# Batches of two for the last units, later routing steps in the tail, and 24 units behind thirteen groups in place of 20 behind twelve

## What is computed

```
x = x + layernorm(attention(layernorm(x)))
logits = layernorm(x) @ Wg;  the two best of 8 experts per token, weights by softmax of the two
out_e  = relu(xn @ W1[e] + b1[e]) @ W2[e] + b2[e]
x = x + layernorm(sum over the two experts of weight_e * out_e)
```

## Time and profile before

| | us |
|---|---|
| median of 3 runs | 921.08 |
| lowest, highest | 917.64, 922.35 |
| the profiled execution | 916.07 |
| its span, first to last instruction | 914.3 |
| TensorE busy | 807.3 (88%) |
| VectorE busy | 750.5 (82%) |
| ScalarE busy | 666.7 (73%) |
| GpSimd busy | 531.4 (58%) |

### The profile page before, as it was taken

One profiled execution on the slowest core, in us unless ns is written; L12 is line 12 of the kernel. 1 busy time (PEld: TensorE's weight loads), 2 busy tenths in 40 slices (PEclk: granted clock), 3 DMA queues, 4 the chain that ended last, 5 costly groups with the idle time before them and its releaser, 6 DMA issues.

```text
span 914.3 us, 25168 instructions
## 1 busy us (share of the span) xinstructions
PE 807.3 (88%) x8010; PEld 681.0 (74%) x8010; DVE 750.5 (82%) x2262; ACT 666.7 (73%) x1629; POOL 531.4 (58%) x1026
## 2 busy tenths in 40 slices
PE   4599999999999999999999999997868799999990
PEld 2487787777777777777777777776658689999990
DVE  5677887999989899998989899888857658888881
ACT  4678887777878677787867778785456678777771
POOL 4244363455556556555655555563656767777775
PEclk9899999999999999999999999999979999999996
DMA  7100000010102021130103000000244366667640
GB/s 197 31 3 4 4 4 12 6 32 10 44 9 58 12 64 56 35 91 9 28 16 88 14 8 11 9 12 8 56 125 139 109 174 180 186 179 189 182 119 1
DMA packets 60301, 57.46 MB, mean 63 GB/s; under 512 B 17863, under 2 KB 43997, under 8 KB 60171
## 3 DMA queue, kind: packets, MB, share of 16 engines
q1 hardware_dynamic: 55211, 47.27, 19.9%
q0 software_dynamic: 4960, 8.58, 2.8%
HBM read 44.14 MB, written 19.99 MB: 70 GB/s over the span
## 4 chain that ended last, share of the span: by engine, by line
DVE 33%; PE 23%; issue 21%; POOL 13%; ACT 3%; DMA 3%; SPq 3%; POOLq 1%; DVEq 0%; another core or an unknown queue 0%; ACTq 0%
POOL out_dram L2243 6%; DVE mg L1050 5%; PE bank L878 5%; DVE xt L788 5%; POOL moe_y L2238 3%; DMA rows<-csplit 2%; DVE state L1077 2%; PE bank L675 2%; DVE y L1062 2%; PE bank L862 2%; DVE ob L1103 2%; SPq L1729 2%; PE bank L677 2%; PE bank L676 2%; DVE y L1059 2%
## 5 line engine op out<-in xcount | busy, mean ns | idle before, releaser
L1041 POOL TENSOR_TENSOR y<-y,zt 128x256 f32<-128x256 f32 x64 | 46.8, 732 | 185.7 <-issue 92.8
L962 ACT ACTIVATE m<-bank 128x512 f32<-128x512 f32 x128 | 69.1, 592 | 77.9 <-PE bank L864 77.8
L675 PE MATMUL bank<-thi,whi 128*128 128x512 f32 x224 | 105.2, 470 | 15.3 <-DVE cs L812 8.3
L2150 PE MATMUL bank<-moe_w,moe_hid 128*128 x728 | 108.0, 278 | 0.0
L2243 POOL DMA_INDIRECT out_dram<-moe_y,moe_token x91 | 91.2, 1003 | 20.6 <-issue 10.5
L2113 PE MATMUL bank<-moe_h_turned,moe_w_now 128*128 128x128 f32 x728 | 99.3, 281 | 0.0
L2150 PEld LDWEIGHTS bank<-moe_w,moe_hid 128*128 128x128 f32 x728 | 97.3, 194 | 0.0
L1050 DVE TENSOR_TENSOR mg<-bank,m 128x512 f32<-128x512 f32 x128 | 82.3, 685 | 17.3 <-PE bank L878 16.6
L2113 PEld LDWEIGHTS bank<-moe_h_turned,moe_w_now 128*128 128x128 f32 x728 | 91.4, 197 | 0.0
L2124 ACT ACTIVATE moe_hid<-bank,moe_w_now 128x128 f32<-128x128 f32 x224 | 63.9, 368 | 35.6 <-PE bank L2113 28.6
L677 PE MATMUL bank<-thi,wlo 128*128 128x512 f32 x224 | 89.6, 400 | 0.0
(11 more groups left out here) (260 smaller groups left out, 2356.4 us busy)
## 6 DMA issues: line engine op xcount, KB each, us to landing
moe_w_now<-pair_weights SPq DMA_DIRECT2D x91, 259.0 KB
moe_block_in<-pair_rows SPq DMA_DIRECT2D x91, 66.5 KB, 2.5
pair_weights<-in_L_ffn_W_dram SPq DMA_DIRECT2D x31, 128.0 KB
parts<-csplit SPq DMA_DIRECT2D x128, 4.0 KB
rows<-csplit SPq DMA_DIRECT2D x128, 4.0 KB
pair_rows<-spare_row SPq DMA_DIRECT2D x29, 66.5 KB
out_dram<-moe_y,moe_token POOLq DMA_INDIRECT x91
pair_rows<-xall,row_index POOLq DMA_INDIRECT x64, 2.6
```

What stands on the lines that cost most here:

```text
L675: PE.matmul(bank[:], whi[:, w], thi[:], start=True, stop=False)
L2150: mm = PE.matmul(o, hid[:, u % HID, k, n, :], w2[:, bass.ds(e, 1), n, :].rearrange("p o d -> p (o d)"), start=False, stop=n == FB - 1, ski ...
```

## The change

Six things change.

1. `SPLIT` is 13 in place of 12, and `EARLY` follows: 24 in place of 20. Group 12's four scatters count for the first share. Group 12's places step now also brings out the counts, and the first table is made from them where it was made before.
2. Group 13's `first` and `second` leave the last tile of the attention part and stand in `dve_tail` step 0; its places product moves to `pe_tail` step 2, its index to `dve_tail` step 2.
3. In the tail VectorE does group 14's `dve_post2` first; group 15's comes at step 2 in place of 3, and GpSimd's `pool_post2` and group 13's scatter at step 1 in place of 3. Group 15's turn comes a step earlier, its places at step 11 in place of 12, its index at 12 in place of 13, its scatter at step 12 in place of 13; the second table is made at steps 12 and 13.
4. VectorE takes the hidden layer of every second unit from unit 15 on (`BY_ACT`), before from unit 21 on.
5. From unit 84 (`FINE`) on the batches are of two units (84-85, 86-87, 88-89, and 90 alone), before 84-87 and 88-90. Their token numbers are made at the first unit's step, not two later.
6. From step 89 on norm and return run six steps behind in place of seven: step 89 takes two units.

```diff
-SPLIT = 12
+SPLIT = 13
 HALVES = ((0, SPLIT), (SPLIT, GROUPS))
 UNITS = (TOK + NPAIR * (P - 1)) // P
 EARLY = -(-(SPLIT * GT - NPAIR * (P - 1)) // P) // 4 * 4
...
         elif q == GROUPS - 3:
-            for step, when in zip(steps, ((g, 1), (g, 2), (g, 2), (g, 3), (g, 3), (g, 3), (g, 3), end, end)):
+            for step, when in zip(steps, ((g, 1), (g, 2), (g, 2), (g, 3), (g, 3), end, end, end, end)):
...
     def dve_tail(dve, step):
         if step == 0:
-            dve_route_index(dve, GROUPS - 3)
             dve_post2(dve, G_LAST - 1, static)
-        if step == 1:
+            dve_route_first(dve, GROUPS - 3)
+            dve_route_second(dve, GROUPS - 3)
             dve_post1(dve, G_LAST, 1, static)
             dve_post1_stats(dve, G_LAST)
+        if step == 1:
+            dve_route_stats(dve, G_LAST - 1)
         if step == 2:
-            dve_route_stats(dve, G_LAST - 1)
-        if step == 3:
             dve_post2(dve, G_LAST, static)
+            dve_route_index(dve, GROUPS - 3)
...
-        if step == 13:
+        if step == 12:
             dve_route_index(dve, G_LAST)
     def pool_tail(pl, step):
         if step == 0:
             pool_post2(pl, G_LAST - 1)
             pool_scatter_group(pl, GROUPS - 4)
-        if step == 3:
+        if step == 1:
             pool_post2(pl, G_LAST)
             pool_scatter_group(pl, GROUPS - 3)
...
-        if step == 13:
+        if step == 12:
             pool_scatter_group(pl, G_LAST)
...
+    BY_ACT = 14
     STEPS = -(-UNITS // 2)
-    QUADS = -(-UNITS // 4)
+    FINE = UNITS // 4 * 4 - 4
+    STARTS = list(range(0, FINE, 4)) + list(range(FINE, UNITS, 2)) + [UNITS]
+    QUADS = len(STARTS) - 1
...
     def by_act(u):
-        return u < EARLY or u % 2 == 0
+        return u < BY_ACT or u % 2 == 0
...
+    SHARES_AT = {STARTS[q]: q for q in range(QUADS)}
+    TOKENS_AT = {STARTS[q] + (2 if STARTS[q] < FINE else 0): q for q in range(QUADS)}
+    def normed_at(step):
+        return range(max(0, step - NORM_LAG + (step > FINE + 5)), min(UNITS, step - NORM_LAG + 1 + (step >= FINE + 5)))
...
-            if u in (13, 14):
-                dve_table(dve, 1, u - 13)
-            if u == 17:
+            if u in (12, 13):
+                dve_table(dve, 1, u - 12)
+            if u == 20:
                 dve_skip(dve, 1)
...
-        for u in range(UNITS + NORM_LAG + 1):
+        for u in range(UNITS + NORM_LAG):
             if u < UNITS:
                 att.pool_tail(pl, u)
-            if u % 4 == 2 and u // 4 < QUADS:
-                pool_tokens(pl, u // 4)
-                pool_share_sums(pl, u // 4)
-            if NORM_LAG <= u < UNITS + NORM_LAG:
-                pool_out(pl, u - NORM_LAG)
-            if u > NORM_LAG:
-                pool_return(pl, u - NORM_LAG - 1)
+            if u in TOKENS_AT:
+                pool_tokens(pl, TOKENS_AT[u])
+                pool_share_sums(pl, TOKENS_AT[u])
+            for v in normed_at(u):
+                pool_out(pl, v)
+                if v:
+                    pool_return(pl, v - 1)
+        pool_return(pl, UNITS - 1)
```

More of the change, by code:

```diff
@@ L1562, in tensor_program @@
         pe_out_tile(pe, T_LAST, T_LAST % 2, last=True)
-        fr = tail_front()
-        pe_route_places(pe, GROUPS - 3, fr)
     def tail_front():
@@ L1628, in pe_tail @@
         fr = tail_front()
-        if step == 1:
+        if step == 2:
+            pe_route_places(pe, GROUPS - 3, fr)
             pe_route_turn(pe, G_LAST - 1, fr)
@@ L1632, in pe_tail @@
             pe_route_logits(pe, G_LAST - 1, fr)
-        if step == 5:
+        if step == 4:
             pe_route_turn(pe, G_LAST, fr)
@@ L1637, in pe_tail @@
             pe_route_logits(pe, G_LAST, fr)
-        if step == 12:
+        if step == 11:
             pe_route_places(pe, G_LAST, fr)
@@ L1646, in act_tail @@
         if step == 1:
-            act_route_turn(act, G_LAST - 1, fr)
-        if step == 2:
             for k in range(2):
                 act_ln2(act, G_LAST, k)
+        if step == 2:
+            act_route_turn(act, G_LAST - 1, fr)
         if step == 3:
@@ L1654, in act_tail @@
                 act_route_scale(act, G_LAST - 1, k)
-        if step == 6:
+        if step == 5:
             act_route_turn(act, G_LAST, fr)
@@ L1664, in dve_tail @@
         if step == 0:
-            dve_route_index(dve, GROUPS - 3)
             dve_post2(dve, G_LAST - 1, static)
-        if step == 1:
+            dve_route_first(dve, GROUPS - 3)
+            dve_route_second(dve, GROUPS - 3)
             dve_post1(dve, G_LAST, 1, static)
             dve_post1_stats(dve, G_LAST)
+        if step == 1:
+            dve_route_stats(dve, G_LAST - 1)
         if step == 2:
-            dve_route_stats(dve, G_LAST - 1)
-        if step == 3:
             dve_post2(dve, G_LAST, static)
+            dve_route_index(dve, GROUPS - 3)
         if step == 4:
             dve_route_first(dve, G_LAST - 1)
+            dve_route_second(dve, G_LAST - 1)
         if step == 5:
-            dve_route_second(dve, G_LAST - 1)
-        if step == 6:
             dve_route_stats(dve, G_LAST)
@@ L1681, in dve_tail @@
             dve_route_index(dve, G_LAST - 1)
+            dve_route_first(dve, G_LAST)
         if step == 9:
-            dve_route_first(dve, G_LAST)
-        if step == 10:
             dve_route_second(dve, G_LAST)
-        if step == 13:
+        if step == 12:
             dve_route_index(dve, G_LAST)
@@ L1700, in pool_tail @@
             pool_scatter_group(pl, G_LAST - 1)
-        if step == 9:
             pool_route_norm(pl, G_LAST)
-        if step == 13:
+        if step == 12:
             pool_scatter_group(pl, G_LAST)
@@ L1834, in in_quad, with quad_with, in_quad_at @@
     def in_quad(q):
-        return range(4 * q, min(4 * q + 4, UNITS))
+        return range(STARTS[q], STARTS[q + 1])
+    def quad_with(u):
+        return u // 4 if u < FINE else FINE // 4 + (u - FINE) // 2
+    def in_quad_at(u):
+        return u - STARTS[quad_with(u)]
     def last_of(q):
@@ L2163, in pool_tokens @@
         pl.wait_ge(skip_ready.sem, 1 if last_of(q) < EARLY else 2)
-        PL.tensor_tensor(token_f[:, a:a + many], skip[:, 4 * q:4 * q + many], v[:, :, C_TOK], ALU.add
+        PL.tensor_tensor(token_f[:, a:a + many], skip[:, STARTS[q]:STARTS[q + 1]], v[:, :, C_TOK], ALU.add
                          ).then_inc(token_kept.sem, 1)
@@ L2266, in tensor_program @@
             att.pe_tail(pe, u)
-            if u == 17:
+            if u == 18:
                 pe_skip(pe)
@@ L2295, in scalar_program @@
                     act_h(act, u + 4)
-                if u % 4 == 0:
-                    act_shares(act, u // 4)
-            if NORM_LAG <= u:
-                act_norm(act, u - NORM_LAG)
+                if u in SHARES_AT:
+                    act_shares(act, SHARES_AT[u])
+            for v in normed_at(u):
+                act_norm(act, v)
             if u in ROOT_AT:
```

17 lines of the change are left out of this document (8 added, 9 removed).

## The result

The changed kernel took 930.2 us (median of 4, 926.8 to 933.15) against 919.4 for the kernel before (median of 4). The two medians differ by 10.8 us; by the comparison of all runs the change takes 1.013 times as long [1.010, 1.016]. The forecast was 925.7, 4.6 us more than before; its range ended at 931. The profiled execution took 932.3 us with a span of 930.5; before it was 914.3.

What follows compares the result with a forecast made beforehand. Full pace is set by TensorE; the first 22 units mostly lose time waiting, and GpSimd alone ends the kernel. Start +12.8, early units -8.6, end +0.45 gave +4.6 us: 925.7, range 916.5 to 931.

Steps and rivals of the forecast that it cites:

- Part 1: Start of the expert units: the first share waits for group 12's scatters, first up product 12.8 us later (12.1 to 13.1).
- Part 2: Early units 0 to 22: they take 60.4 us against 69.03 before, 8.6 less.
- 12 to 22: Stretch from unit 12's to unit 22's up product: 24.7 us against 31.94, with unit 20's wait gone.
- 10 to 12: Stretch from unit 10's to unit 12's up product: 7.0 us, between 4.90 and 8.02 by whether ScalarE's pause recurs.
- 0 to 8: Stretch from unit 0's to unit 8's up product: 23.8 us against 24.17, as group 14's turn moves into a wait.
- The floor: Second share's first load 51.0 us after the first up product, so unit 22 starts 55.9 after it at the earliest.
- part 2's floor was too low: Sign at the second share's start: to be concluded if TensorE still waits for rows at unit 22.
- Part 3: Kernel's end, GpSimd working without pause: batches of two add 0.45 us, bounds -0.8 and +1.7.
- VectorE becomes the bound: Slower rival, from unit 15: VectorE's tables, mixes and hidden layers hold the units; +8.6, 929.7 us; chance 0.17.
- The floor's rival: Rival, early units: pauses don't recur and the second share's earliest start decides; +0.1, 921.2 us; chance 0.2.
- the faster one: Rival, early units: the whole early chain tightens; -4.8, 916.3 us; chance 0.13 together with the undelayed start.
- the start is not delayed: Rival, start of the units: the first load stays where it was; -10.7 us; chance under 0.03.

Runs made afterwards that it cites:

- split13_alone: Kernel before with 13 groups and 24 units in the first share, nothing else changed: 938.0 us, 1.021 of before.
- split12_rest_kept: Changed kernel with 12 groups and 20 units in the first share again, the rest of the change kept: 917.8 us, 0.998 of before.
- twelve_groups_early_loads: Changed kernel with 12 groups and 20 units again, the second share's first five loads ahead of unit 19's weights: 914.6 us, 0.997 of before.
- second_loads_early: Changed kernel with the second share's first five row loads ahead of unit 20's weights, not behind unit 23's: 932.8 us, 1.014 of before.
- hidden_by_scalare: Changed kernel with ScalarE making the hidden layer of all 24 units of the first share: 933.6 us, 1.016 of before.
- extra_scatters: Kernel before with ten more GpSimd indirect writes: four at unit 40, four spread over units 56 to 59, two at 74: 934.6 us, 1.016.
- write_kinds: Kernel before with four plain GpSimd-queue writes at unit 40 and four indirect writes of 128-byte rows at unit 64: 927.2 us, 1.011.
- changed_again: Changed kernel run once more, unaltered, for a second profile of its early units: 932.4 us, 1.016 of before.

## Why the prediction was wrong, step by step

**Part 1 was right, and nearly so in size.** I took the first product 12.8 us later. Counted from attention's end, it is 12.7 later in the first profile (25.3 against 12.6), 14.2 in the second and 12.8 to 14.4 in the three others with the same start. The load follows the fourth scatter's start by 3.29 (I took 3.49), the product its weights by 2.82 (I took 3.17). The estimate of 2.6 by the Trainium skill ("DMA: Bandwidth & Descriptors", "Anatomy of one DMA") was nearer, 0.22 too low; that section gives its fit for DMAs from GpSimd's queue, and this load is SyncE's. By that estimate the sum would have been 0.6 lower, not the 0.7 that I wrote. split13_alone and split12_rest_kept show that the start passes into the time nearly whole.

**Part 2 failed, and it is most of the miss.** I let 8.6 us be repaid. In the first profile units 0 to 22 repay nothing and take 3.5 more, in the second they repay 3.8. All profiles of kernels with thirteen groups have 65.0 to 72.6 us there, against 69.0 before and 60.4 forecast. In the first profile this is 12.2 us too long, where the whole end comes 11.9 later than the sum has it (16.5 in place of 4.6). In the second, counted from attention's end, 7.8 us are missed: 4.8 here, 1.4 in the start and 1.7 in units 22 to 28.

Three rows of the kernel before that I had not read for it, the fourth scatters of groups 14 and 15 on GpSimd and ScalarE's copy of a turn behind the latter:

```profile
706.87 0.96 POOL L1376 DMA_INDIRECT pair_rows<-xall,row_index  x1 [0.31 <-DVE pair L1315]
...
724.84 0.96 POOL L1376 DMA_INDIRECT pair_rows<-xall,row_index  x1 [0.30 <-issue]
```

```profile
728.15 0.38 ACT L2066 ACTIVATE moe_h_turned<-bank 128x256 f32<-128x256 f32 x1 [1.71 <-remote]
```

- *12 to 22, 24.7 forecast, 27.6 to 31.6 measured.* This is the step that failed. "Unit 20's wait is gone" was read as a gain of its own length and that of its slow products, with three pairs of units at 4.3 behind it. But before, the scatters of group 15 (the fourth at 724.84) already made TensorE's signals late: the turn that ended at 724.92 was up at 728.13, ScalarE was idle for 1.71 us until 728.15, and the wait for rows until 731.08 came right behind. With twelve groups and the rows' wait taken away (twelve_groups_early_loads), the stretch falls from 31.6 (split12_rest_kept) to 28.8 only, and the pause stands alone, 4.18 us long. The forecast has no term for group 15's pause and the low clock behind it.
- *10 to 12, 7.0 forecast, 6.8 to 7.5 measured (8.2 in split13_alone).* Right, but for want of a cause I treated the 3.57 of the earlier trace rows as a chance event. It ends 1.8 us behind the start of group 14's fourth scatter (706.87); the pauses of the other groups end 1.7 to 5.1 us behind theirs. Had I laid GpSimd's timeline beside ScalarE's, I would have seen such a pause behind groups 13, 14 and 15.
- *0 to 8, 23.8 forecast, 25.0 in most profiles, 28.7 in the first.* Group 13's scatters (696.03 to 699.94) make a pause there, for which I had no term. The 28.7 comes with 10 us of low clock, which not every execution has.
- *The floor was computed from the wrong gate.* I put the second share's first load at S + 51.0, from the last scatter. It went out at S + 68.5, since SyncE has it behind the weights of unit 23, and these wait for unit 17's down product. second_loads_early confirms this order. Cost: 1.3 us in units 22 to 28, 1.7 in the second profile, where ScalarE waits 1.09 us for rows until 757.37; by my own signs that is "part 2's floor was too low".

**Part 3 was right**: 0.45 forecast, 0.40 in the changed kernel and 0.34 alone.

**The rivals.** "VectorE becomes the bound" named nearly the right time (929.7) for a wrong reason: hidden_by_scalare takes the work away from it and wins nothing. That its time fits is luck. That rival's price, a pause with slow products behind it at about 4 us, was of the right kind; such pauses come with the groups' scatters and not from VectorE. The floor's rival (921.2) and the faster one (916.3) wanted the pauses gone or shorter; they were there in every profile. That the start is not delayed is refuted by the load at 678.23.

## What to carry to other kernels

A wait moved to the head of a chain costs its whole length, unless a row shows slack behind it; a repayment that is put together from many small waits needs a cause for each of them. When several engines stop at once though the one they name had finished, lay all timelines side by side, the DMA-issuing engine's too, before you call the pause random. And look for what lies under a wait before you count its removal as a gain.

## What the runs showed of the hardware

- Four indirect writes of 128 rows by GpSimd, 1.27 us apart, made TensorE's signals to other engines up to 7.2 us late and cost 7.8 to 8.6 us each time at full pace, with 532 bytes or 128 a row. Four with a pair of out and return between them (2.9 to 5.9 us apart) cost 7.2. Four plain writes from GpSimd or SyncE and 5 us of GpSimd's arithmetic cost nothing; two indirect writes in a row made one gap of 0.68 us and cost 0.9.
- Only TensorE's signals are seen late. In the changed kernel, extra_scatters and write_kinds no signal of ScalarE, VectorE or GpSimd that the traces hold was up more than 0.6 us behind its instruction in the expert part.
- Behind most such gaps of TensorE the granted clock was at its lower level for 3.4 to 10.2 us (705 to 715 above; 6.8 us at unit 40 with the added scatters), in which eight products take 1.92 us in place of 1.06. So a pause is mostly paid for twice. Behind groups 13 and 15 of changed_again the clock did not fall.
- Attention's end came between 661.4 and 668.2 us in all these profiles, 661.4 and 666.9 in the two of the changed kernel, so starts should be compared from there.
